# A two-layer decoder: local attention re-ordered, and in relative attention the sum and the maximum fused per head, with two turns moved

## What is computed

```
# local attention: 16 heads of size 8, one shared key and value head
qp  = (q @ Wq) / sqrt(8);  k, v = split(kv @ Wkv)
# blocks of 64 positions; each query sees the previous, its own and the next block
attn = qp . k_extended ;  probs = softmax(attn, 3*64 keys)
out  = (probs . v_extended) @ Wc

# relative attention: 16 heads of size 8, 128 keys
q, k, val = heads(x @ Wq + bq), heads(x @ Wk + bk), heads(x @ Wv + bv)
content_score = (q + u) . k
pos_score     = relative_shift((q + v) . pos)
weights = softmax((content_score + pos_score) / sqrt(8))
out = (weights . val) @ Wo + bo
```

## Time and profile before

| What | Value |
|---|---|
| median of 3 runs | 1704.16 us (1703.48 to 1704.88) |
| the profiled execution's own time | 1704.72 us |
| its span in the trace | 1702.9 us |
| TensorE (PE) busy | 1349.3 us, 79% |
| VectorE (DVE) busy | 1075.6 us, 63% |
| ScalarE (ACT) busy | 886.8 us, 52% |
| GpSimd (POOL) busy | 617.7 us, 36% |
| mean granted TensorE clock | 0.927 |

### The profile page before, as it was taken

The page is one execution under the profiler, slowest core; times in us unless marked ns, Lnnn a source line. Parts: engine busy times, 40 slices in busy tenths (PEclk is TensorE's granted clock), DMA queues, the critical chain, the costliest instruction groups (busy, mean ns, idle before and its releaser), DMA issues. The chain is left out here.

```text
span 1702.9 us, 41561 instructions
## 1 busy us (share of the span) xinstructions
PE 1349.3 (79%) x12665; PEld 859.1 (50%) x12727; DVE 1075.6 (63%) x3090; ACT 886.8 (52%) x1709; POOL 617.7 (36%) x901
## 2 busy tenths in 40 slices
PE   2499999985888888875674888878787595998998
PEld 0155555553555555544542555555554493554554
DVE  2377777763565665645533888888887515776674
ACT  1277777762666666662323566767675223222321
POOL 4367767731212222211001566666661321121120
PEclk9999999995999999998995999999999556999999
DMA  4000000000000000000003566666666000000000
GB/s 143 1 2 2 0 0 0 1 2 1 2 2 0 0 0 0 0 2 1 0 1 87 145 166 186 170 176 175 171 186 171 1 0 1 7 7 8 11 7 13
DMA packets 147219, 78.57 MB, mean 46 GB/s; under 512 B 6673, under 2 KB 146066, under 8 KB 147010
## 3 DMA queue, kind: packets, MB, share of 16 engines
q1 hardware_dynamic: 146610, 75.45, 16.3%
q0 software_dynamic: 528, 2.10, 0.4%
HBM read 41.62 MB, written 35.91 MB: 46 GB/s over the span
## 5 line engine op out<-in xcount | busy, mean ns | idle before, releaser
L715 POOL TENSOR_TENSOR rr<-ms_eps,minus_half 128x16 f32<-128x16 f32 x64 | 184.8, 2905 | 92.6 <-DVE ms_eps L926 92.6
L1047 DVE TENSOR_REDUCE rowmax<-psum 128x4 f32<-128x768 f32 x128 | 122.5, 957 | 111.7 <-PE psum L1942 111.5
L469 PE MATMUL psum<-identb,stacks 128*128 128x128 bf16 x1800 | 146.0, 227 | 49.3 <-DVE stacks L462 21.6
L469 PEld LDWEIGHTS psum<-identb,stacks 128*128 128x128 bf16 x1800 | 108.4, 101 | 89.6 <-DVE stacks L462 31.4
L560 PE MATMUL psum<-probsT,values 128*32 128x128 f32 x2048 | 110.4, 287 | 45.4 <-DVE attn L586 44.9
L965 DVE TENSOR_REDUCE rowmax<-psum 128x4 f32<-128x512 f32 x128 | 88.2, 689 | 61.3 <-PE psum L1821 60.2
L476 ACT ACTIVATE qT<-psum 128x1024 bf16<-128x1024 bf16 x96 | 99.5, 1036 | 30.8 <-PE psum L469 30.8
L1766 ACT ACTIVATE pos_rows<-psum 128x512 f32<-128x512 f32 x72 | 43.0, 597 | 129.7 <-PE psum L2278 124.0
L1644 ACT ACTIVATE probsT<-psum 128x512 f32<-128x512 f32 x128 | 78.0, 609 | 45.0 <-PE psum L2147 45.0
L436 POOL CAST stacks<-staged 128x384 bf16<-128x384 f32 x87 | 58.3, 670 | 103.4 <-PE psum L469 54.4
L511 POOL TENSOR_TENSOR rstd<-vareps,minus_half 128x1 f32<-128x1 f32 x96 | 53.4, 556 | 113.5 <-DVE vareps L411 111.6
(11 more groups left out here) (243 smaller groups left out, 3458.1 us busy)
## 6 DMA issues: line engine op xcount, KB each, us to landing
skew<-pos_rows SPq DMA_DIRECT2D x128, 258.0 KB, 4.6
pos_score<-skew SPq DMA_DIRECT2D x128, 256.0 KB, 4.1
X<-in_x_dram POOLq DMA_DIRECT2D x1, 2048.0 KB, 12.1
ctxT<-in_ctx_dram SPq DMA_DIRECT2D x1, 2048.0 KB, 10.9
out_dram<-X SPq DMA_DIRECT2D x8, 256.0 KB, 2.3
w_up<-in_L_ffn_w_e_dram SPq DMA_DIRECT2D x2, 512.0 KB, 4.2
w_down<-in_L_ffn_w_e_dram SPq DMA_DIRECT2D x2, 256.0 KB, 6.1
consts<-in_consts_dram SPq DMA_DIRECT2D x1, 401.0 KB, 3.2
```

The source lines that it names most:

```text
L469: last = pe.transpose(turned[:, t, :], stacks[:, which, 2 * t:2 * t + 2, :].rearrange("s h k -> s (h k)"), identb[:, :])
L715: pool.tensor_tensor(out=rr[:, par, i * H:(i + 1) * H], in0=ms_eps[:, i * H:(i + 1) * H], in1=minus_half[:, 0:H], op=ALU.pow).then_inc(A.r ...
L1047: dve.tensor_reduce(rowmax[:, par, first:first + 2 * PT - 1:2].rearrange("s (b h) -> s b h", b=2), B.max_space, AX.X, ALU.max, negate=True ...
```

## The change

1. **Relative attention, VectorE.** `add_max` no longer adds a round as one 128x512 instruction and reduces it with a second. For each of the four heads one `tensor_tensor_reduce` adds 128 columns and gives their maximum. `take_max` waits for `P.add`; the semaphore `P.mx` is gone; one `sem_inc` on a spare semaphore stands between the waits and the first instruction.
2. **Relative attention, order.** `turn_xn` and `save_xnT` of sequence b+4 at the end of an iteration become those of b+3 near the start of the next (`turn_normed`). `turn_q2(b+2)` moves ahead of `project` and `turn_less(b, 1)`, its copy `save_q2T` ahead of `exps_turned(b, 1)`. `turn_out` moves ahead of `project`, `output` ahead of `position_score(b+2, 1)`. VectorE's list is re-ordered.
3. **Local attention.** `turn_again` writes the layer norm's bank (`ln_bank`) and waits for `B.v`, no longer for `B.qT`; the next `turn_xn` waits for `B.again` in its turn. `turn_out` moves ahead of `project`; the scores of round 2 ahead of `weigh(b, 0)`, of round 3 ahead of `score_turned(b, 2)`; `weigh(b, 3)` ahead of `score(b+2, 0)`. On VectorE `key_rest_of` moves ahead of `residual_y`.

```diff
-        def turn_stack(pe, q, which, sem):
+        def turn_stack(pe, q, which, sem, to=None):
-            turned = q.head_bank.bitcast(BF16).rearrange("k (t s) -> k t s", s=S)
+            turned = (q.head_bank if to is None else to).bitcast(BF16).rearrange("k (t s) -> k t s", s=S)
...
 # relative attention, VectorE
-                    dve.tensor_tensor(summed[:, r % 2, :, :], P.score_bank[r % 2],
-                                      pos_score[:, par, r * PT:(r + 1) * PT, :], ALU.add).then_inc(P.add, 1)
-                    wait(dve, P.add, n * R + r + 1)
                     wait(dve, P.less, n * R + r - 1)
-                    dve.tensor_reduce(topmost[:, r % 2, :], summed[:, r % 2, :, :], AX.X, ALU.max).then_inc(P.mx, 1)
+                    dve.sem_inc(k0.carry, 1)
+                    for p in range(PT):
+                        last = dve.tensor_tensor_reduce(summed[:, r % 2, p, :], P.score_bank[r % 2][:, p, :], pos_score[:, par, r * PT + p, :],
+                                                        1.0, -3.0e38, ALU.add, ALU.max, topmost[:, r % 2, p:p + 1])
+                    last.then_inc(P.add, 1)
                 def take_max(n, r):
-                    wait(dve, P.mx, n * R + r + 1)
+                    wait(dve, P.add, n * R + r + 1)
                 def body(b, par, left):
                     take_max(b, 1)
+                    if left >= 4:
+                        ln_stats(dve, P, b + 4, b + 4)
+                    if later:
+                        normalise(dve, P, b - 1)
+                    add_max(b, par, 2)
+                    take_max(b, 2)
                     if left >= 3:
                         stage_query(b + 3, Q2)
                         stage_query(b + 3, Q)
-                    add_max(b, par, 2)
-                    if later:
-                        normalise(dve, P, b - 1)
-                    take_max(b, 2)
-                    if left >= 3:
                         stage_key_value(b + 3, 1 - par)
                     add_max(b, par, 3)
-                    if left >= 4:
-                        ln_stats(dve, P, b + 4, b + 4)
                     take_max(b, 3)
+                    if left >= 1:
+                        add_max(b + 1, 1 - par, 0)
                     if later:
                         residual_y(dve, P, b - 1)
...
 # relative attention, ScalarE
                     exps_turned(b, 0)
+                    if left >= 3:
+                        save_xnT(act, P, b + 3, xnT[:, :], P.proj, b + 3)
+                    if left >= 2:
+                        save_q2T(b + 2)
                     exps_turned(b, 1)
                     if left >= 2:
-                        save_q2T(b + 2)
                         save_rows(b + 2, par, 0)
...
 # relative attention, TensorE
+                def turn_normed(n):
+                    wait(pe, P.x, n - 4)
+                    turn_xn(pe, P, n, P.vst, n)
                     score(b, par, 2)
+                    if later:
+                        turn_out(pe, P, b - 1)
+                    if left >= 3:
+                        turn_normed(b + 3)
+                    if left >= 2:
+                        turn_q2(b + 2)
                     if left >= 3:
                         project(b + 3)
-                    if later:
-                        turn_out(pe, P, b - 1)
                     turn_less(b, 1)
...
-                    if left >= 4:
-                        if later:
-                            wait(pe, P.x, b)
-                        turn_xn(pe, P, b + 4, P.vst, b + 4)
...
 # local attention, TensorE
-                def turn_again(n, par, turned_before):
+                def turn_again(n, par, valued):
                     wait(pe, B.nm, 2 * n + 2)
-                    wait(pe, B.qT, turned_before)
-                    turn_stack(pe, B, par, B.again_ps)
+                    wait(pe, B.v, valued)
+                    turn_stack(pe, B, par, B.again_ps, B.ln_bank)
+                def turn_normed(n):
+                    wait(pe, B.again, n - 1)
+                    turn_xn(pe, B, n, B.v, n)
                         score(b + 1, 1 - par, next_four, 1)
-                    if left >= 2:
-                        project(b + 2)
                     if later:
                         turn_out(pe, B, b - 1)
+                    if left >= 2:
+                        project(b + 2)
+                    if left >= 1:
+                        score(b + 1, 1 - par, next_four, 2)
                     weigh(b, four, 0)
                     weigh(b, four, 1)
...
+                    if left >= 1:
+                        score(b + 1, 1 - par, next_four, 3)
                     score_turned(b, par, four, 2)
                     score_turned(b, par, four, 3)
-                    if left >= 1:
-                        score(b + 1, 1 - par, next_four, 3)
                     score_sums(b, par, four, 1)
...
                         turn_again(b + 1, 1 - par, b + 3 if left >= 2 else NB)
+                    weigh(b, four, 3)
                     if left >= 2:
                         score(b + 2, par, after_four, 0)
-                    weigh(b, four, 3)
                     if left >= 3:
-                        turn_xn(pe, B, b + 3, B.v, b + 3)
+                        turn_normed(b + 3)
```

More of the change, by code:

```diff
@@ L305, in decoder @@
         [P.proj, P.q2, P.q, P.k, P.split, P.vst, P.v, P.bias, P.q2T_ps, P.q2T, P.qT_ps, P.qT, P.kT_ps, P.kT,
-         P.e, P.es, P.s, P.add, P.mx, P.less, P.p, P.pT_ps, P.o, P.on, P.aT_ps, P.aT,
+         P.e, P.es, P.s, P.add, P.less, P.p, P.pT_ps, P.o, P.on, P.aT_ps, P.aT,
          P.y, P.x, P.bqs, P.zeroed, P.pos] = sems(
-            "d", "proj q2 q k split vst v bias q2T_ps q2T qT_ps qT kT_ps kT e es s add mx less p pT_ps o "
+            "d", "proj q2 q k split vst v bias q2T_ps q2T qT_ps qT kT_ps kT e es s add less p pT_ps o "
             "on aT_ps aT y x bqs zeroed pos")
@@ L1236, in body @@
                     if left >= 1:
-                        add_max(b + 1, 1 - par, 0)
+                        take_max(b + 1, 0)
+                        add_max(b + 1, 1 - par, 1)
                     if left >= 4:
                         ln_apply(dve, P, b + 4, b + 4)
-                    if left >= 1:
-                        take_max(b + 1, 0)
-                        add_max(b + 1, 1 - par, 1)
                 dve.wait_ge(ld.d, LOADS_D)
@@ L1584, in cross_attention @@
                     save_queries(n, n)
+                save_again(0, 0)
                 save_xnT(act, B, 2, xnT[:, :], B.proj, 2)
-                save_again(0, 0)
                 body_quads(act, body)
@@ L2022, in cross_attention @@
                 for n in range(2):
-                    turn_xn(pe, B, n, B.v, n)
+                    turn_normed(n)
                     project(n)
@@ L2031, in cross_attention @@
                 score(1, 1, 1, 0)
+                turn_normed(2)
                 body_quads(pe, body)
@@ L2160, in body @@
                     weigh_values(pe, P, b, par, 0)
-                    if left >= 2:
-                        turn_q2(b + 2)
                     turn_less(b, 2)
@@ L2173, in body @@
                         score(b + 1, 1 - par, 0)
+                    if later:
+                        output(pe, P, b - 1, w_o1[:, :])
                     if left >= 2:
                         position_score(b + 2, 1)
-                    if later:
-                        output(pe, P, b - 1, w_o1[:, :])
                     turn_less(b, 3)
```

22 lines of the change are left out of this document (7 added, 15 removed).

## The result

The changed kernel takes 1640.16 us (median of 4 runs, 1635.95 to 1644.88) against 1704.52 us for the kernel before (4 runs, 1703.48 to 1709.24): ratio 0.9622, 95% interval 0.9600 to 0.9644. Forecast were 1651 us and 53 us of gain; measured are 64.4 us.

A forecast was written before the change was run, and what follows sets the result against it. Relative attention was taken as bound by a loop through VectorE and TensorE, local attention mainly by TensorE. Gains of 34 + 19 = 53 us off the profiled 1704.7 us gave a median of 1651 us, range 1634 to 1692.

The forecast's parts named there:

- F: Relative attention, VectorE: total of a round's four fused 128-column instructions, taken as 1.05 us, bounded by 0.80 and 2.3.
- I take one more fixed share: Relative attention: each fused instruction costs 0.20 us plus another 0.063 us for its second output, 0.263 us in all.
- The lower bound of 0.80: Relative attention: the fused form costs nothing extra, so a round is 4 x 0.20 = 0.80 us.
- The tail in front of the subtraction: Relative attention: take_max right behind add_max in rounds 2 and 3 exposes the last fused instruction's tail, 0.18 us each.
- The chain of relative attention: TensorE and ScalarE chain laid out from outT: an iteration falls from 12.0 to 10.75 us, with seams 34 us gained.
- a seam or two of sem_inc: Relative attention: VectorE's added queue instruction costs nothing to 0.25 us per iteration; 0.12 us taken off the gain.
- the prediction's own slope: Relative attention: an iteration takes 10.75 + 2 x (F - 1.05) us until VectorE's own sum, 5.5 + 4F, is larger.
- Local attention: 10.31 forecast: Local attention: new order and bank shorten an iteration from 10.94 to 10.31 us, 19 us over 30; bounds nothing and 1.4.
- Half-rate fused instruction: Rival, relative attention: half-rate or poorly overlapped fused instructions, F = 1.6, iteration 11.9 us, total 1682 us; chance 0.2.
- Local attention gains nothing: Rival: the chain save_again, xn turn, xnT, outT, exponentials replaces local attention's wait; total 1670 us; chance 0.14.
- Shifted scores late: Rival, relative attention: shifted scores land late under more DMA load, half the stage's gain lost; 1668 us; chance 0.06.
- Slower by full exposure: Rival, relative attention: fused instructions and second outputs fully exposed, F = 2.3, iteration 14.7 us, total 1766 us; chance 0.1.

The follow-up runs named there:

- the parts alone: Three runs on the kernel before: local attention's change only, 1670.48 us; relative attention's new order only, 1688.60 us; fused sum and maximum only, 1688.04 us.
- order only: The kernel before with only relative attention's new order, sum and maximum still two instructions of 512 columns: 1688.60 us, ratio 0.9926.
- The fusion alone: The kernel before with only the fused sum and maximum of relative attention, in the old order: 1688.04 us, ratio 0.9906.
- q2T copy late: The changed kernel with turn_q2 back behind weigh 0 and save_q2T back behind the exponential of round 1: 1707.31 us, ratio 1.0021.
- thin cast: The changed kernel with GpSimd's second cast of a split (L441) done for the first of 16 heads only: 1645.59 us, ratio 0.9664.

## Why the prediction was right, and where it was off

**The bound and its shape: right.** A loop through both engines in relative attention, TensorE's two waits in local attention, no interplay of the stages: the parts alone show each. The waits changed as the prediction asked (the two waits of the earlier trace rows and the two of the earlier trace rows gone, VectorE idle before a round's sum waiting for score, though 1.4 us and not about 1). GpSimd's later splits cost nothing, as foretold: its idle time before L436 is 2.5 us an iteration. Nor did the shifted scores come late: they land after 3.0, 4.2 and 5.5 us (least, median, most; the earlier trace rows had 3.1, 4.1, 5.8), with the DMA share at 0.70 instead of 0.65.

**F, the cost of a round: too high, 1.05 taken, 0.85 measured.** The step that failed is "I take one more fixed share". The instructions start 0.21 us apart, against 0.20 for plain ones: the accumulator's read costs 0.01 us, not 0.063, though its row says 0.08. The lower bound of 0.80 was the better value. The tail in front of the subtraction, put at 0.18, came to 0.11 (0.96 less 0.85). The Trainium skill's "VectorE: DVE Perf Modes", section "Two Vector instructions with no wait between them", says that an operation which writes out its accumulator is two instructions; the trace agrees, with 512 rows of each kind. The Trainium skill's "Vector Engine (DVE) Microarchitecture Reference", section "Points that are easy to get wrong", says that the scalar-tensor-tensor layout runs at half the throughput with two non-bf16 sources in SBUF; with one source in PSUM nothing of that kind shows at 0.21 us for 128 columns, and no run here has both in SBUF with the accumulator on.

**The chain of relative attention: 10.75 forecast, 11.08 measured.** Up to `weigh 0` the layout held, even a little early, in the iteration shown: the xnT copy started 1.52 after outT (1.67 forecast), project 1.85 (2.06), weigh 0 3.46 (3.67). Then the subtraction of round 2. It was to end at 3.87 with F = 1.05, so at 3.47 with the F measured, and ended at 4.19 (1058.98 less 1054.79), 0.72 late; turn_less followed at 4.25, position_score at 5.20 instead of 4.87. The next iteration, one of the shorter, does a little better (changed kernel, timeline):

```profile
1065.98 0.59 ACT L567 ACTIVATE outT<-psum 128x512 f32<-128x512 f32 x1
...
1068.30 0.29 DVE L1210 CUSTOM_DVE_ANT_0 summed<-psum,pos_score 128x128 f32<-128x128 f32 x1
...
1070.96 0.39 PE L2135 MATMUL psum<-posT,q2T 48*128 48x128 bf16 x4
```

Its position_score starts at 4.98. From there to the next outT both take 5.99 us, where the layout had 5.88 and the kernel before 5.87. So of the 0.33 us that the mean is too long, 0.22 lie ahead of position_score, with the late subtraction, and 0.11 behind it, where the 0.1 that the moved output and xn turn were to give did not come. The failed sentence is "With F = 0.8 it stays at 10.75, since the chain does not shorten". The run with `ln_stats` moved bears this out: with 0.72 us less on VectorE's list ahead of it, position_score starts 4.76 us after outT (4.85 in the other iterations), at or ahead of the layout's 4.87, and the iteration takes 10.80 on the mean. For the longer iteration the rows show 0.57 of the 0.72:

- The first fused instruction of round 1 starts 0.23 us after its score ends (1053.57 to 1053.80), where the plain sum, in the run with the order only, starts 0.04 after it (1105.98 to 1106.02): 0.19.
- 0.24 us of idle time stands before the fused instruction of round 2 (1057.33), where VectorE had waited for nothing: 0.24. This gap is there in every second iteration only; in the one after it the instruction follows at once (1068.30), and that is the whole difference of 11.19 and 10.97.
- The subtraction of round 1 takes 0.83 instead of 0.69 (0.89 in the shorter iteration), beside GpSimd's L441 and L443: 0.14.

The rest of 0.15 I did not trace for certain. A candidate: the score of round 1 now ends 1.22 us before outT starts (1053.57 and 1054.79), and in the kernel before it ended 1.46 before it (1104.99 + 0.39, and 1106.84), since the xn turn and its copy stood between; the prediction does not say which it used. The first two gaps are what the prediction called "a seam or two of sem_inc", with a row bound of nothing to 0.25 us and 0.12 taken; they came to 0.43 and 0.19 in turn, 0.31 on the mean. The runs with the two forms of add_max agree: between order only (11.55) and the changed kernel (11.08), the loop's two rounds should save 2 x (1.32 - 0.85) = 0.94 and pay these 0.31 and 0.17 for the longer subtraction (0.68 with the order only), which leaves 0.46; measured 0.47. What makes the gaps is only bounded. Neither is the wait for `P.less`. The order alone has neither. The fusion alone has one of 0.22 us before round 0 but none before round 2 (1114.82, right behind stage_query), so the 0.24 us are seen only with the fused form in its new place behind `normalise`. Whether it is the sem_inc or the custom instruction itself was not tried apart.

The two errors pull against each other: with the F of 1.05 and the same gaps the iteration would have been 11.08 + 2 x 0.20, some 11.5 us (an estimate by the prediction's own slope). That the stage gained 29.5 us where 34 were forecast is partly luck.

**Local attention: 10.31 forecast, 9.84 measured.** Here the mechanism was right and two terms off. From save_again on, the layout held to the output product within 0.15 us (xn turn at 1.27 for 1.15, turn_out 2.59 for 2.50, weigh 0 4.50 for 4.37, output 6.20 for 6.14). But the sums' exponential ended at 8.77 and not 9.05, because `score_turned` started at 6.64, beside score 3 (598.09 and 598.10), where I had it wait until score 3 was done at 7.05. The mean over the stage puts score 3 before it at a loss of 0.15 all the same, as the run with it put back shows. And turn_again started at 9.18, before the modelled end of weigh 2 (600.64 against 600.72), where I had put 0.12 us of seam behind it: 0.20. The kernel before had shown as much in relative attention, where a turn starts 0.06 us before the modelled end of `weigh_values` (1110.63 + 0.42):

```profile
1110.99 0.62 PE L469 MATMUL psum<-identb,stacks 128*128 128x128 bf16 x8
```

Together 0.47 an iteration, and 31.9 us instead of 19, still inside the stated bounds of nothing and 1.4 an iteration.

**The rivals.** Half-rate fused instruction (1682 us): F = 1.6 against 0.85 measured, out. Local attention gains nothing (1670): out; the longer chain of save_again, xn turn and outT is there, with 0.3 us of wait, and does not bind. Shifted scores late (1668): out, by the landing times. Slower by full exposure (1766): out for the real instruction; the run with the instruction twice shows that the mechanism is real, since a round of 1.70 us brings 12.59 at full clock.

**The sum.** 29.5 + 31.9 = 61.4 us against 34 + 19 = 53, with one term too large by 4.5 and one too small by 12.9. The forecast of 1651 was 11 us above the median, the range held it, and the error that decides is the local one. The upper end of the range, 1692, does not follow from the F = 1.7 named with it (12.3 us an iteration loses 9 us, half of the local gain gives 9.5 back: 1704); it belongs to F = 1.6. The result lies far from that end.

## What to carry to other kernels

When two parts of a change shorten one loop through two engines, cost them together: alone they gave 12 and 11 us, together 29.5. A chain laid out by hand should be laid out on every engine's queue, with each queue's own gaps; the step that I had down as "the chain does not shorten" went through another engine's list, and moving 0.7 us of statistics off that list was worth 7.5 us. For seams, take the smallest that the trace shows between the same two kinds of instruction, not one typical value.

## What the runs showed that I had not expected

**The granted clock.** Relative attention ran at 1.00 before and at 0.99 after, but at 0.83 with the fused instruction twice and at 0.75 to 0.87 (stretches of 40 us, from 1000 us on) with the q2T copy late. It was no chance of one execution: over the whole program all four executions with the copy late were granted 0.889 to 0.894, the changed kernel 0.926 to 0.929. With the copy late TensorE was busy 21.05 of 24 us at full clock up to 984 us, was granted 0.50 (the 1.2 GHz level) from 990 to 996 us, where it was busy throughout, and came back only in part. TensorE was busy 81% before, 92% after, and 88% in that stretch before the fall, so busy share alone does not order the cases. Such an iteration costs 13.5 to 16 us instead of 11.7 to 12.6, a larger loss than what the change brings an iteration. What sets it off stays open. It also means that a variant's total says little of its edit until the clock of its stages has been read.

**VectorE and GpSimd hold each other up.** The subtraction, which reads two SBUF tiles, lasts 0.69 us alone and up to 0.94 beside a GpSimd instruction that started first; when it started first, GpSimd's was the longer one (changed kernel, timeline):

```profile
1051.68 0.69 DVE L1216 TENSOR_TENSOR summed<-summed,topmost 128x512 f32<-128x512 f32 x1
1051.78 0.84 POOL L441 CAST stacks<-rest 128x256 bf16<-128x256 f32 x1 [0.17 <-POOL rest L438]
...
1060.61 0.40 POOL L441 CAST stacks<-rest 128x256 bf16<-128x256 f32 x1 [0.17 <-POOL rest L438]
1060.65 0.90 DVE L1216 TENSOR_TENSOR summed<-summed,topmost 128x512 f32<-128x512 f32 x1
```

The Trainium skill's "SBUF — State Buffer", section "SBUF: two separate sides", gives the first of the two an exclusive lock on a shared port for its whole instruction. Who waits agrees; the size does not quite, since VectorE lost 0.21 us where GpSimd's copy still had 0.36 to go. The thin cast took part of it away and gained nothing: the one subtraction that it freed, that of round 3, was off the path or had slack behind it. The one that lies on the path, that of round 1, it did not free.
